# Building the head of a graph kernel: fewer list steps, turned rows loaded, low bits made later

## The reference

```
layer 0:  msg = (x[src] + rel_emb[clip(type, 0, 63)]) @ W_msg.T + b_msg
          x1  = layernorm(x + x @ W_self.T + b_self + segment_sum(msg, dst) / max(deg, 1))
layer 1:  h   = swish(mean(x1[src]) @ W1_l.T + b1 + x1 @ W1_r.T)
layer 2:  out = layernorm(x1 + mean(h[src]) @ W2_l.T + b2 + h @ W2_r.T)
```

## Time and profile before

| | us |
|---|---|
| median of three runs | 366.36 |
| the profiled execution | 366.51 |
| its span | 364.7 |
| TensorE busy (share) | 335.0 (92%) |
| VectorE busy | 232.8 (64%) |
| ScalarE busy | 173.9 (48%) |
| one ACT_TABLE_LOAD of ScalarE (x3) | 1.3 |

### The profile page before, as it was taken

How to read it: one execution, slowest core, us unless ns; L and a number is a source line. 1 busy time by engine, 2 the same in 40 slices (tenths; PEclk the granted TensorE clock), 3 DMA queues, 4 the chain that set the end, 5 groups by cost and what they waited for, 6 DMA issues and landing times.

```text
span 364.7 us, 9187 instructions
## 1 busy us (share of the span) xinstructions
PE 335.0 (92%) x3385; PEld 250.4 (69%) x3385; DVE 232.8 (64%) x597; ACT 173.9 (48%) x385; POOL 4.9 (1%) x17
## 2 busy tenths in 40 slices
PE   0689999999999999999999999999999999999970
PEld 0579998998998998998984454555474455455460
DVE  6999988998999999999446942330345031431454
ACT  1585667769778878778522141331252131121040
POOL 5000000000000000000000000000000000000000
PEclk9999999999999999999999999999999999999997
DMA  4700000000000000000000000000000001100102
GB/s 138 171 2 4 2 2 3 4 2 4 2 2 2 3 4 3 3 2 2 24 16 3 0 0 2 0 2 0 0 2 3 0 1 31 29 2 29 30 2 67
DMA packets 8523, 5.38 MB, mean 15 GB/s; under 512 B 370, under 2 KB 8476, under 8 KB 8476
## 3 DMA queue, kind: packets, MB, share of 16 engines
q1 hardware_dynamic: 8188, 4.32, 4.4%
q10 hardware_dynamic: 288, 0.43, 0.3%
HBM read 3.14 MB, written 1.60 MB: 13 GB/s over the span
## 4 chain that ended last, share of the span: by engine, by line
PE 84%; DVE 8%; ACT 4%; issue 2%; DMA 1%; ACTq 0%; DVEq 0%
PE ps L943 54%; PE ps L891 16%; PE ps L1009 5%; PE ps L1019 3%; PE ps L962 2%; ACT counts L834 2%; DVE hot L1182 1%; PE ps L989 1%; DMA counts<-dst_t 1%; PE ps L898 1%; PE ps L908 1%; DVE hot L1175 1%; DVE table L1192 1%; ACT new_first L812 1%; ACT scaled L790 1%
## 5 line engine op out<-in xcount | busy, mean ns | idle before, releaser
L943 PE MATMUL ps<-counts,table 128*128 128x256 f16 (+2 forms) x1350 | 214.6, 309 | 0.0
L943 PEld LDWEIGHTS ps<-counts,table 128*128 128x128 f16 x1350 | 114.9, 97 | 74.2 <-issue 0.2
L834 ACT CAST counts<-ps 128x494 f32 x208 | 107.7, 578 | 45.5 <-PE ps L891 44.9
L891 PE MATMUL ps<-hot 128*128 128x156 f16 (+1 forms) x584 | 67.9, 241 | 15.6 <-DVE hot L1182 15.0
L891 PEld LDWEIGHTS ps<-hot 128*128 128x128 f16 x584 | 53.1, 103 | 17.3 <-DVE hot L1182 15.3
L1182 DVE TENSOR_TENSOR hot<-iota,edges 128x1200 f16<-128x1200 f16 x73 | 56.6, 775 | 0.0
L1175 DVE TENSOR_TENSOR hot<-iota,edge_rows 128x768 f16<-128x768 f16 x73 | 40.1, 550 | 4.9 <-PE ps L928 4.6
L898 PE MATMUL ps<-window_hot,hot 128*128 128x19 f16 x292 | 42.5, 181 | 0.0
L1272 DVE TENSOR_TENSOR new_first<-ps,scaled 128x512 f32<-128x512 f32 (+1 forms) x9 | 5.4, 600 | 54.0 <-ACT scaled L790 54.0
L1272 DVE TENSOR_TENSOR hot<-ps,scaled 128x512 f32<-128x512 f32 (+1 forms) x8 | 5.1, 639 | 41.6 <-ACT scaled L790 41.6
L898 PEld LDWEIGHTS ps<-window_hot,hot 128*128 128x128 f16 x292 | 28.9, 99 | 0.7
(11 more groups left out here) (135 smaller groups left out, 320.3 us busy)
## 6 DMA issues: line engine op xcount, KB each, us to landing
table<-x SPq DMA_DIRECT2D x2, 768.0 KB, 5.1
out<-new_first SPq DMA_DIRECT2D x3, 256.0 KB
out<-hot SPq DMA_DIRECT2D x3, 256.0 KB, 2.4
counts<-first_dst ACTq DMA_DIRECT2D x1, 208.0 KB, 3.9
counts<-dst_t SPq DMA_DIRECT2D x1, 208.0 KB, 4.5
counts<-type_t ACTq DMA_DIRECT2D x1, 208.0 KB, 4.7
counts<-src_t SPq DMA_DIRECT2D x1, 208.0 KB, 5.0
hot<-w_l SPq DMA_DIRECT2D x2, 64.0 KB, 2.0
```

The lines of the kernel that those rows point to most:

```text
L834: nc.scalar.copy(A[:, HALVES[half], bass.ds(bases[group % 8], GROUP_W)], window(group, half)).then_inc(copied[half], 1)
L891: return nc.tensor.matmul(window(group, half)[:, :, at[t]], row(tiles[t], LOW_AT, P), blocks_of(tiles[t], half), start=group == half == t ...
L943: last = nc.tensor.matmul(ps[:, sums_bank(q), first:first + width], table[:, b, part, :], A[:, b, at:at + width], start=b == part == 0, st ...
```

## The change

- The lists: `place` is a clamp of (first dst of the tile minus base), `offset` is taken from `FROM_BASE` and `place`, and the clamp of the types is made by ScalarE with two Relus.
- x comes from a host array laid out by partition, relation rows included (`x_rows`); a second one holds x turned (`x_turned`). SP loads its chunks into `own_T` and `sum_first` in turns, each behind the product that read the place before. `turn` and `turn_out` remain for layers 1 and 2 alone.
- own(0) to own(3) go behind groups 6, 8, 10 and 17, the stores behind 15, 18, 19 and 20.
- The low bits are made in 7 pieces behind groups 10 to 16. The third slot starts at group 14. The constants are made behind groups 4, 14 and 21.
- Part 0 takes its 25 high products first, then the low ones in the order of the pieces. It starts behind group 11 and waits for `x_lo` product by product.
- `spread()` counts products instead of blocks.

```diff
-THIRD_SLOT = 12
...
-CONSTANT = 4
...
+THIRD_SLOT = 14
...
-TURN = [5 + 2 * k for k in range(POSTED)]
-OWN = [7 + 2 * k for k in range(POSTED)]
+OWN = (6, 8, 10, 17)
+STORED = (15, 18, 19, 20)
...
+OWN_BANKS = (6, 7, 5)
...
+LOW_PIECES = ((16, 19), (19, 22), (22, 25), (0, 4), (4, 8), (8, 12), (12, 16))
+LOW_FROM = 10
+LOW_LATE = 3
...
+def products_of(part):
+    if part:
+        return [(b, which) for b in range(BLOCKS) for which in range(2)]
+    return [(b, 0) for b in range(BLOCKS)] + [
+        (b, 1) for first, end in LOW_PIECES for b in range(first, end)]
...
-        room = 0 if group in OWN else 4
+        room = 0 if group in OWN else 8
...
-            count = min(max(room, 0), BLOCKS - block)
...
+            count = min(max(room, 0), 2 * BLOCKS - at)
...
-                    waiting += [(group + 2, k, 2, (0, 1)), (group + 3, k, 2, (2, 3))]
+                    waiting += [(group + 2, k, 4, (0, 1)), (group + 3, k, 4, (2, 3))]
                 else:
-                    waiting += [(group + 1, k, 3, ())]
-                    waiting += [(group + 3 + t, k, 3, (t,)) for t in range(SUB)]
...
+                    waiting += [(group + 2 + t, k, 6, (t,)) for t in range(SUB)]
...
+        def x_T(q):
+            return sum_first[:] if q < POSTED and q % 2 else own_T[:]
...
-            return ps[:, (dense_bank(0), DEG)[q % 2], :].rearrange("p (t d) -> p t d", d=D)
+            return ps[:, OWN_BANKS[q % 3], :].rearrange("p (t d) -> p t d", d=D)
...
+            def load_turned(q):
+                first = q * CHUNK
+                sp.dma_start(x_T(q)[:, 0:nodes_of(q)], x_turned[:, first:first + nodes_of(q)]
+                             ).then_inc(turned_in[q % 2], 16)
...
-            sp.dma_start(stage_x[:, 0:BLOCKS // 2, :],
-                         x[0:cut, :].rearrange("(b p) d -> p b d", p=P)).then_inc(x_in[0], 16)
-            sp.dma_start(stage_x[:, BLOCKS // 2:BLOCKS - 1, :],
-                         x[cut:full, :].rearrange("(b p) d -> p b d", p=P)
-                         ).then_inc(x_in[1], 16)
-            sp.dma_start(stage_x[REL_ROW:P, BLOCKS - 1, :], rel_emb).then_inc(x_in[1], 16)
-            sp.wait_ge(pads_zero, 1)
-            sp.dma_start(stage_x[0:N - full, BLOCKS - 1, :], x[full:N, :]).then_inc(x_in[1], 16)
+            cut = BLOCKS // 2
+            for half, span in enumerate((slice(0, cut), slice(cut, BLOCKS))):
+                sp.dma_start(stage_x[:, span, :].rearrange("p b d -> p (b d)"),
+                             x_rows[:, span.start * D:span.stop * D]).then_inc(x_in[half], 16)
+            load_turned(0)
...
+            load_turned(1)
+            for q in range(2, EARLY):
+                sp.wait_ge(dense_done, q - 1)
+                load_turned(q)
+            sp.wait_ge(dense_done, EARLY)
+            load_turned(EARLY)
...
+            sp.wait_ge(dense_done, EARLY + 1)
+            load_turned(EARLY + 1)
...
+            act.wait_ge(type_in, 16)
+            act.wait_ge(constants, 1)
+            below = type_i.bitcast(F32)
+            nc.scalar.activation(below, type_i, ACT.Relu, bias=most_type[:], scale=-1.0
+                                 ).then_inc(type_step, 1)
+            act.wait_ge(type_step, 1)
+            nc.scalar.activation(edge_row[:, :, 0, :], below.rearrange("p (h t) -> p h t", t=PAIR),
+                                 ACT.Relu, bias=most_type[:], scale=-1.0).then_inc(type_step, 1)
...
-                act.wait_ge(turned, q + 1)
-                if q:
-                    act.wait_ge(dense_done, q)
-                nc.scalar.copy(own_T[:, 0:nodes], ps[:, turn_bank(q), 0:nodes]
+                act.wait_ge(turned, q + 1 - CHUNKS)
+                act.wait_ge(dense_done, q)
+                nc.scalar.copy(own_T[:, 0:nodes], ps[:, TURN, 0:nodes]
...
-                    if group == TURN[k]:
-                        turn_out(k)
...
-                if not opens:
+                if CHUNKS < q and not opens:
                     turn_out(q)
...
+            def aggregate_part(part, first, end):
+                q, at = part // 2, part % 2 * PART
+                if first == 0 and end:
+                    if part < EARLY_PARTS:
+                        wait_copied(pe, READY[part])
+                    if part == 0:
+                        pe.wait_ge(x_hi, X_PIECES)
+                    elif at == 0:
+                        pe.wait_ge(sum_ready, q)
+                for k in range(first, end):
+                    b, which = products_of(part)[k]
+                    if part == 0 and which:
+                        pe.wait_ge(x_lo, low_piece(b) + 1)
+                    last = nc.tensor.matmul(
+                        ps[:, sums_bank(q), at:at + PART], table0[:, b, which, :],
+                        A[:, b, part * PART:(part + 1) * PART], start=k == 0,
+                        stop=k + 1 == 2 * BLOCKS, skip_group_check=True)
+                if first < end == 2 * BLOCKS and at:
+                    last.then_inc(agg_done, 1)
...
-                if q:
-                    pe.wait_ge(own_ready, q)
+                if q == CHUNKS:
+                    pe.wait_ge(weights_ready, 3)
                 else:
-                    pe.wait_ge(weights_ready, 1)
-                if q < POSTED:
-                    pe.wait_ge(x_lo, (chunk_of(q) * SUB + SUB - 1) // X_PIECE + 1)
-                elif turn_bank(q) == messages_bank(q - 1):
-                    pe.wait_ge(messages_scaled, q)
+                    pe.wait_ge(own_ready, q - CHUNKS)
...
-                pe.wait_ge(own_ready, q + 1)
-                pe.wait_ge(weights_ready, 3)
-                if q > 1:
-                    pe.wait_ge(own_stored, q - 1)
+                wait_turned(q)
+                pe.wait_ge(weights_ready, 1)
+                if q > 2:
+                    pe.wait_ge(own_stored, q - 2)
...
-                    last = nc.tensor.matmul(own_rows(q)[:, t], own_T[:, t * P:(t + 1) * P],
+                    last = nc.tensor.matmul(own_rows(q)[:, t], x_T(q)[:, t * P:(t + 1) * P],
...
-                    pe.wait_ge(own_ready, max(q + 1, POSTED))
+                    if q == 0:
+                        pe.wait_ge(own_stored, POSTED)
+                    if q >= CHUNKS:
+                        pe.wait_ge(own_ready, q - CHUNKS + 1)
+                    elif q >= POSTED:
+                        wait_turned(q)
...
-                    if group == TURN[k]:
-                        turn(k)
...
-                part, blocks = BEHIND[group]
-                if len(blocks):
-                    if 0 in blocks:
-                        wait_copied(pe, READY[part])
-                        pe.wait_ge(x_lo, X_PIECES)
-                    aggregate(part // 2, blocks, part % 2 * PART, PART)
-            aggregate(EARLY, range(LEFT[1], BLOCKS), 0, PART)
+                aggregate_part(*BEHIND[group])
+            aggregate_part(EARLY_PARTS - 1, LEFT[1], 2 * BLOCKS)
             wait_copied(pe, GROUPS)
             open_bank(dense_bank(EARLY))
-            aggregate(EARLY, range(BLOCKS), PART, PART)
-            turn(EARLY)
+            aggregate_part(EARLY_PARTS, 0, 2 * BLOCKS)
             count_degrees(EARLY)
             aggregate(EARLY + 1, range(BLOCKS))
             dense(EARLY, all_tiles(EARLY))
-            turn(EARLY + 1)
             count_degrees(EARLY + 1)
...
-            nc.vector.scalar_tensor_tensor(by_tile(start_i), of_groups(), float(MOST_SHIFT),
-                                           by_tile(first_i), ALU.add, ALU.min).then_inc(prep, 1)
+            nc.vector.tensor_tensor(by_tile(start_i), by_tile(first_i), of_groups(), ALU.subtract
+                                    ).then_inc(prep, 1)
             nc.vector.tensor_tensor(by_tile(edge[:, FROM_BASE, :]), by_tile(dst_i), of_groups(),
                                     ALU.subtract).then_inc(prep, 1)
             dve.wait_ge(prep, 2)
-            nc.vector.tensor_tensor(by_tile(start_i), by_tile(start_i), of_groups(), ALU.max
-                                    ).then_inc(prep, 1)
+            nc.vector.tensor_scalar(place_i[:].rearrange("p g t -> p (g t)"), start_i, 0,
+                                    MOST_SHIFT, ALU.max, ALU.min).then_inc(place_ready, 1)
             nc.vector.tensor_tensor(next_node[:, 0:early], by_tile(dst_i)[:, 0:early, GROUP - 1],
                                     base_i[:, 1:GROUPS], ALU.is_equal).then_inc(prep, 1)
-            dve.wait_ge(prep, 4)
-            nc.vector.tensor_tensor(place_i[:], by_tile(start_i), of_groups(), ALU.subtract
-                                    ).then_inc(place_ready, 1)
-            nc.vector.tensor_tensor(offset_i, dst_i, start_i, ALU.subtract).then_inc(prep, 1)
             dve.wait_ge(src_in, 16)
             nc.vector.tensor_scalar(block_i, src_i, P.bit_length() - 1, None,
                                     ALU.arith_shift_right).then_inc(prep, 1)
-            dve.wait_ge(prep, 7)
+            dve.wait_ge(prep, 3)
+            dve.wait_ge(place_ready, 1)
```

(51 more changed lines are left out.)

67 lines of the change are left out of this document (34 added, 33 removed).

## The result

The changed kernel takes 361.19 us, median of 4 runs (361.0 to 362.44). The kernel before took 366.39 beside it (4 runs, 366.32 to 367.38). The ratio is 0.9883 (0.985 to 0.9916): 1.2% faster. Run again in five rounds it took 361.06 (6 runs) against 366.22 (11 runs), ratio 0.9868 (0.9848 to 0.9889). The profiled execution took 361.31 (span 359.5), 5.2 us under that of before.

The account below looks back on a forecast made before the run. VectorE was taken to set the head and TensorE the middle. Terms -2.3 -0.7 -0.7 -0.3 -0.46 +0.5 +0.5 = -3.5 us took 366.5 to 363.0, by the median 362.9; range 361.7 to 365.4.

Parts of the forecast that it names:

- the 21.9 us: VectorE's summed work for groups 10 to 21, bounding that stretch over TensorE's 19.0 us; count(22) 2.3 us earlier, at 50.3.
- Shorter lists, -1.1: List chain in the head: ends at 9.62 instead of 10.75, 1.1 us off the path; ScalarE's two Relus cost nothing.
- Loads, 0: Loads of x, turned x, weights and last bias: no cost taken, bounds 0 and +1.0 us.
- Groups 0 to 8, count(8) at 26.0: Head without low pieces and turns, at the low clock: count(8) ends at 26.0, 3.9 us ahead, mostly lent.
- Rival 2: Head: TensorE's clock rises early if counts without holes lift it; about -1.0, 361.9 us; 10%.
- The additions, +0.5 and +0.5: Unpriced small hand-overs up to group 22, +0.5 (0 to 0.9); clock rising mid own(1), about 27 us, +0.5.
- Six products earlier -0.7, groups 94 to 97 -0.3: Group 25 lacks six products, -0.7 us; at groups 94 to 97 ScalarE's own_T copy is gone, -0.3 (0 to -0.5).
- Four left over in place of ten, -0.7: Behind group 93: 4 products left over in place of 10, -0.7 us.
- seam, -0.46: Seam to layer 1: own_T copy leaves the chain, root starts 0.46 us earlier, all of it coming through.
- The later clock (1, 3): Clock rises in own(2) or first products, 364.1 to 365.2 us, 25%; or stays low into part 0, slower, 8%.
- All lent time kept back (4): VectorE's stretch costs 2 us more and the head's gain is gone by group 22: 365.0 us; 7%.
- mid-build stall took the shift (5): Stalls in the middle and at groups 94 to 97 absorb the shift, leaving the seam and a bit: 366.0; 5%.

Follow-up runs that it names:

- new_lists: The kernel before with the new list steps alone, types clamped by ScalarE's two Relus: 365.21 us against 365.86 for before, ratio 0.9993, not told apart.
- warm_before: The kernel before with 22 matmuls of 512 columns in front of its first group: 365.4 us, ratio 0.9984, not told apart.
- low_early: The changed kernel with the seven low pieces behind groups 3 to 9 in block order, in place of 10 to 16: 361.17 us, ratio 0.9874.
- holes: The changed kernel with a memset of zeros on VectorE behind each of groups 3 to 7, to give TensorE holes back: 362.21 us, ratio 0.9907.
- best1: The changed kernel with three stores behind groups 22 to 24, low pieces two groups earlier and 22 matmuls before the first group: 360.19 us, ratio 0.9849.
- block_order: The changed kernel with part 0 in block order, high and low products by turns, low pieces left late: 363.18 us, ratio 0.9937.
- old_lists: The changed kernel with the list work of the kernel before, VectorE's clamp of the types included: 361.95 us, ratio 0.9898.
- early_low_late_stores: The changed kernel with the last three stores behind groups 22 to 24 and low pieces behind groups 8 to 14: 360.82 us, ratio 0.986.
- late_stores: The changed kernel with the last three stores behind groups 22, 23 and 24 in place of 18, 19 and 20: 360.12 us, ratio 0.9847.

## Why the prediction was right, and where it was not

*Which engine is the bound, and where.* Right in the main. VectorE is full from hots(10) to hots(22) (20.00 of 20.00 us in the table), and the 21.9 us were met to 0.01. The path leaves it at hots(20), not at hots(21), and runs through TensorE's work from there. That TensorE waited 1.1 us and not 2 to 3 fits this: it had less to spare than the 2.9 us of the forecast. The terms of the 21.9 were met too: a low piece of 3 blocks 0.47 from start to start and of 4 blocks 0.60, a store 0.60, and a group's hots 1.17.

*Shorter lists, -1.1.* Right: next_hot starts at 9.68 (forecast 9.62), 1.07 earlier. The offset from an f16 and an int32, for which there was no row, cost the 0.50 taken. The two Relus run at 6.22 and 6.89, 0.64 and 0.66 long, with no table load ahead of them. The Trainium skill ("ScalarE: Activation LUTs", section "Table sets: the hidden batching unit") says that relu is in every set, and the trace agrees. On the clock the other rule of the Trainium skill that the prediction weighed ("TensorE: Matmul & The Clock Gate", section "What's actually happening"), that activity releases the throttle, pointed the right way. The level was up at 15.5 and 20.6 us in the two profiles of the kernel after. But new_lists, with the holes of before, had it at 15.4 too; it fell again in the head in seven of the fourteen profiles; and the warming matmuls of warm_before held it for two groups in the profiled execution. So the trace agrees with that rule only in part.

*Loads, 0.* Right. No list step and no group waits for x, the weights or the last bias. The halves of x land 6.0 and 4.2 us after issue. The last turned load is issued at 185.19 and isn't waited for.

*Groups 0 to 8, count(8) at 26.0.* This is the step that failed, in one term: the clock from own(0) on. The forecast adds 1.92 for own(0) and twice 1.36 for the groups behind it, all at the lower level. From own(0)'s start to the end of count(8) they took 0.96, 0.9 and 1.2, 1.6 us less, because the clock was up. In the kernel after a 156-column matmul goes from 0.18 us start to start down to 0.10 to 0.12 at 15.5 us, in its second profile at 20.6. The forecast had put the rise at about 27 us, in the middle of own(1), and added +0.5 for it. It made the clock wait for a dense piece, since in the kernel before it was up only behind own(0). Rival 2 gave 361.9 with 10%; it was the nearest, 0.7 us above the result. That the clock rose early is shown; that it did so because the holes are gone, as rival 2 says, is not (new_lists).

*Up to own(0)* the number is right and the reason is not. Count(6) ends at 21.45, and the steps as forecast give 21.37 (12.8, six groups at 1.36, next_hot 0.41), which is TensorE's pace at the lower level. The clock was up for four of these groups, and they took 1.3 to 1.6 us each all the same, since ScalarE's copies closed three of them, with VectorE 0.2 to 0.3 us ahead of them at count(5). The forecast had said that ScalarE doesn't hold them. In the second profile, with the clock low until 20.6, TensorE waits 0.53 for VectorE at group 4, goes on at its own 1.34 us for group 5, and count(6) ends 9.11 us behind ScalarE's first copy, as in the first profile. So two sums came out nearly the same, and that the forecast's was exact is luck. No run took the pieces of x out of the head, so what would be won by it is open.

*The additions, +0.5 and +0.5.* Neither was needed. The hand-overs weren't there (VectorE's stretch closes to 0.01), and the second is the clock again. The 1.5 us earlier start and this 1.0 make up the 2.3 us by which count(22) is earlier than forecast (48.99 against 51.3), less 0.2 behind hots(22), which took 2.6 to count(22) and not 2.4.

*Six products earlier -0.7, groups 94 to 97 -0.3.* Together they gave less: the shift goes from 3.58 at group 22 to 4.03 at group 102, 0.45 in place of 1.0. It was 4.17 at group 26 and 3.80 at group 27, so the six products were there (0.6) and part was lost again at the next hand-over; at group 95 it is 3.83, so 0.25 of the 0.7 is left. From group 95 to group 97 it grows by 0.33, as forecast, and 0.13 of that is gone by group 102.

*Four left over in place of ten, -0.7; seam, -0.46.* Right: 0.66 and 0.49.

*Rivals 1, 3, 4 and 5.* The later clock (1, 3) didn't come; both profiles of the changed kernel had it up ahead of own(0). All lent time kept back (4) did not happen: 1.9 of 5.5 us were given back. No mid-build stall took the shift (5): it stayed at 3.8 to 4.1 us over 50 groups.

*What each edit is worth, by undoing it.* Lists 0.8 to 0.9 us; high bits first 2.0, given the late pieces; late pieces 0; turns of chunks 0 to 2 in the head 0.4, with overlapping ranges; the seam and what is left over 1.15 by the two profiles. They need not add up, since several act through the same start of hots(10).

*What stays open.* What exactly makes the clock fall. TensorE waited 0.4 to 1.0 us at a time for VectorE ahead of the falls in the head of new_lists, low_early, holes and best1. Block_order waited 0.61, 0.38 and 0.39 there and stayed up, while old_lists with 0.61 and 0.38 and early_low_late_stores with 0.60, 0.37 and 0.19 fell. And how much of before's time is its clock: its runs at the lower level are 3.4 us above after, those at the upper level 5 us. A kernel before with the clock up from the start would settle it; warm_before was meant to be that, and its profiled execution wasn't.

## What to carry to other kernels

When work is moved between two engines' stretches, sum the receiving engine's work from one buffer release to another, from rows: such a sum was good to 0.01 us here, and it also names what to take out next (three stores, 1.0 us at the median, 0.5 at group 22 in the profile). Look too at the other engines ahead of it: ScalarE and VectorE set TensorE's pace in groups 3 to 5 here, which the sum of TensorE's steps hid because it gave the same number. Time won ahead of such a stretch counts only as far as it moves the release that starts it, and work merely pushed from ahead of it into it was worth nothing here. Give the clock's rise its own range, from the first work that could lift it to the last, and ask whether the change fills the holes ahead of it.

## What the runs showed of the hardware

- The granted clock went down again after it had been up: in the head of new_lists to 0.50 over 22 to 28 us, in best1 over 20 to 22, in block_order over 34 to 36 behind a wait of 2.69 us. There 8 products took 1.87 us against 1.03. It fell in the middle of the build as well: 0.57 over 168 to 172 us in warm_before, behind a wait of 0.44 us, which cost 1.5 us.
- The view of stretches writes 1.00 from the start of the program even where the pace is half (own(0) at 1.92 us in the earlier trace rows); it shows only levels behind a first fall. In the head the pace of equal matmuls is the better clock.
- The same kernel comes out at levels 1 to 1.7 us apart: 359.9 to 360.2 and 361.5 for best1, 364.5 and 366.2 for before. The dates of the clock's rise and fall differ between profiles, and one fall cost 1.5 us (warm_before), so they may make these levels. It is not shown, since one run of each was profiled, and late_stores speaks against it as the only cause: its profiled execution is 0.9 us above its other runs without a fall in the head.
- A memset of zeros over 128x640 f16 ran as 320 uint32 columns in 0.33 us, where a low piece over the same place takes 0.82.
